# Masking the scores of the first block's attention with four passes on quarters of the rows

## The reference

```python
q = (x @ wq).reshape(b, n, H, DH)...   # 16 heads of 64
sim = jnp.einsum('bhid,bhjd->bhij', q, k) * SCALE
sim = jnp.where(mask[:, None, None, :], neg, sim)   # mask: 32 x 128, one flag for a key
attn = jax.nn.softmax(sim, axis=-1)
out = jnp.einsum('bhij,bhjd->bhid', attn, v)
```

## Time and profile before

| | us |
|---|---|
| median of 3 executions | 2085.46 |
| lowest, highest | 2080.9, 2087.44 |
| the profiled execution | 2081.89 |
| its span (first to last instruction) | 2080.2 |
| PE busy in the span | 1893.0 (91%) |
| PE's weight loads busy | 1501.7 (72%) |
| DVE, ACT, POOL busy | 1429.1, 1191.3, 498.9 |

### The profile page before, as it was taken

How to read it: one execution, slowest core, us unless ns; L and a number is a source line. 1 busy time by engine, 2 the same in 40 slices (tenths; PEclk the granted TensorE clock), 3 DMA queues, 4 the chain that set the end, 5 groups by cost and what they waited for, 6 DMA issues and landing times.

```text
span 2080.2 us, 47917 instructions
## 1 busy us (share of the span) xinstructions
PE 1893.0 (91%) x17007; PEld 1501.7 (72%) x17007; DVE 1429.1 (69%) x3597; ACT 1191.3 (57%) x3980; POOL 498.9 (24%) x810
## 2 busy tenths in 40 slices
PE   3899999999999999999599999888887788699998
PEld 1788888888888888888367777666665555467776
DVE  5577787777777777777465676478887699354443
ACT  1567676767676666776244544377776566133333
POOL 1021111111111111111221221044444576021110
PEclk8899999999999999999799999899999899599999
DMA  7000000000000000000200000100000000000000
GB/s 225 25 2 2 2 2 2 2 2 2 2 2 2 2 2 2 2 2 2 72 1 1 1 1 1 36 2 3 2 2 9 24 13 2 1 0 11 11 3 19
DMA packets 30226, 25.69 MB, mean 12 GB/s; under 512 B 5276, under 2 KB 26788, under 8 KB 29992
## 3 DMA queue, kind: packets, MB, share of 16 engines
q1 hardware_dynamic: 29992, 22.62, 3.7%
HBM read 20.52 MB, written 2.10 MB: 11 GB/s over the span
## 4 chain that ended last, share of the span: by engine, by line
issue 66%; POOL 15%; PE 10%; POOLq 8%; DVE 1%; DMA 0%; DVEq 0%; ACT 0%
POOL X L1797 3%; POOL work L914 2%; PE bank L1918 2%; PE bank L1905 2%; PE bank L1907 2%; POOL work L1588 2%; POOLq L917 2%; POOL H L918 1%; POOL work L1013 1%; POOL X L1598 1%; PE bank L1885 1%; POOLq L1587 1%; POOL work L902 1%; POOLq L1796 1%; POOLq L1597 1%
## 5 line engine op out<-in xcount | busy, mean ns | idle before, releaser
L679 ACT ACTIVATE work<-bank,work 128x128 f32<-128x128 f32 x1024 | 363.1, 402 | 208.2 <-DVE work L758 208.2
L520 PE MATMUL bank<-work,wbig 128*128 128x128 f32 x2048 | 262.3, 277 | 0.5 <-ACT work L742 0.5
L520 PEld LDWEIGHTS bank<-work,wbig 128*128 128x128 f32 x2048 | 246.0, 193 | 1.2 <-ACT work L742 0.8
L679 ACT ACTIVATION_READ_ACCUMULATOR work<-bank,work 128x1 f32 x1024 | 246.4, 241 | 0.0
L765 DVE TENSOR_TENSOR work<-work 128x512 f32<-128x512 f32 x256 | 177.7, 694 | 19.8 <-issue 0.9
L758 DVE TENSOR_REDUCE work<-bank 128x4 f32<-128x512 f32 x256 | 159.0, 684 | 33.6 <-PE bank L559 33.6
L694 ACT ACTIVATE work<-bank 128x512 f32<-128x512 f32 x256 | 168.7, 660 | 22.8 <-PE bank L533 22.8
L533 PE MATMUL bank<-ident,work 128*128 128x128 f32 x1024 | 157.6, 276 | 11.8 <-DVE work L765 11.8
L533 PEld LDWEIGHTS bank<-ident,work 128*128 128x128 f32 x1024 | 114.2, 140 | 58.7 <-issue 31.3
L912 POOL TENSOR_TENSOR work<-work,lneps 128x1 f32<-128x1 f32 x64 | 15.3, 238 | 580.9 <-DVE work L875 580.9
L2078 DVE TENSOR_TENSOR work<-wff,bank 128x320 f32<-128x320 f32 (+1 forms) x128 | 62.5, 489 | 127.7 <-ACT wff L1993 127.2
(11 more groups left out here) (311 smaller groups left out, 4016.6 us busy)
## 6 DMA issues: line engine op xcount, KB each, us to landing
wbig<-in_moe_w SPq DMA_DIRECT2D x2, 1536.0 KB, 9.3
work<-in_mask_l SPq DMA_DIRECT2D x8, 256.0 KB, 3.0
out<-X SPq DMA_DIRECT2D x8, 256.0 KB, 2.3
H<-in_moe_w SPq DMA_DIRECT2D x3, 512.0 KB, 5.6
wff<-in_moe_w SPq DMA_DIRECT2D x1, 1024.0 KB
X<-in_x SPq DMA_DIRECT2D x1, 512.0 KB, 4.1
wbig<-in_sa_wq SPq DMA_DIRECT2D x1, 512.0 KB, 3.9
wbig<-in_sa_wk SPq DMA_DIRECT2D x1, 512.0 KB, 4.7
```

Of the source, the lines that this page charges most:

```text
L520: last = nc.tensor.matmul(o[:, j * T:(j + 1) * T], w[:, t * 128:(t + 1) * 128], src, start=True, stop=True)
L679: last = nc.scalar.activation(at_probs[:, g, h, :], bank[g][:, h * T:(h + 1) * T], ACT.Exp, bias=at_nmax[:, g, h:h + 1], accum_out=at_den[ ...
```

## The change

The mask passes leave `score` and stand in a function `mask(u)` of their own, called once for a unit ahead of both calls of `score`. It does four passes, one for each of the four banks, each on a quarter of the rows (32 rows from partition 0, 32, 64, 96). The wait for the exponentials of the unit before (`at.probs` at 4u) stands ahead of them; the wait at 4u - 2 goes. For this `onerow` has a row of ones at the head of each quarter (four memsets for two), and `keymask` is filled on all partitions: the two halves of the mask are loaded onto all 128 partitions (two transfers for four), converted by two instructions on 128 partitions (for four on one), and the clearing of `keymask` goes. The rows of `keymask` under the zero rows of `onerow` no longer are zero.

```diff
-        mask32 = [[H[p:p + 1, NB * j:NB * j + NB, :].rearrange("p b d -> p (b d)").bitcast(mybir.dt.int32)
-                   for j in range(2)] for p in (0, DH0)]
-        mask8 = [[m.bitcast(mybir.dt.uint8) for m in pair] for pair in mask32]
+        mask32 = [H[:, NB * j:NB * j + NB, :].rearrange("p b d -> p (b d)").bitcast(mybir.dt.int32) for j in range(2)]
+        mask8 = [m.bitcast(mybir.dt.uint8) for m in mask32]
...
+            def mask(u):
+                b = unit(u)[1]
+                for g in range(GH):
+                    p = 32 * g
+                    nc.tensor.matmul(bank[g][:, :].rearrange("p (h t) -> p h t", h=GH), onerow[p:p + 32, :],
+                                     keymask[p:p + 32, b * T:(b + 1) * T].unsqueeze(1).to_broadcast([32, GH, T]),
+                                     start=True, stop=False, skip_group_check=True)
+
             def score(u, pair):
-                b = unit(u)[1]
-                for odd in range(2):
-                    p = odd * DH0
-                    nc.tensor.matmul(bank[2 * pair + odd][:, :].rearrange("p (h t) -> p h t", h=GH),
-                                     onerow[p:p + DH0, :],
-                                     keymask[p:p + DH0, b * T:(b + 1) * T].unsqueeze(1).to_broadcast([DH0, GH, T]),
-                                     start=True, stop=False, skip_group_check=True)
...
                 if now:
+                    need(pe, at.probs, 4 * u)
+                    mask(u)
                     need(pe, at.q_low_sb, u + 1)
                     need(pe, at.qk_sb, 3 * u + 3)
-                    need(pe, at.probs, 4 * u - 2)
                     score(u, 0)
-                    need(pe, at.probs, 4 * u)
                     score(u, 1)
...
-            for p in range(2):
-                for j in range(2):
-                    load(mask32[p][j], ins["mask"][:, j * B * T // 8:(j + 1) * B * T // 8], "mask")
+            for j in range(2):
+                load(mask32[j], ins["mask"][:, j * B * T // 8:(j + 1) * B * T // 8].to_broadcast([128, B * T // 8]), "mask")
...
             nc.gpsimd.memset(onerow[:, :], 0.0)
-            nc.gpsimd.memset(keymask[:, :], 0.0)
             nc.gpsimd.memset(b2_sb[:, :], 0.0)
             pool.drain()
-            nc.gpsimd.memset(onerow[0:1, :], 1.0)
-            nc.gpsimd.memset(onerow[DH0:DH0 + 1, :], 1.0)
+            for p in range(0, 128, 32):
+                nc.gpsimd.memset(onerow[p:p + 1, :], 1.0)
...
-            dve.wait_ge(loaded["mask"], 64)
-            for p in range(2):
-                for j in range(2):
-                    nc.vector.tensor_scalar(keymask[p * DH0:p * DH0 + 1, j * B * T // 2:(j + 1) * B * T // 2],
-                                            mask8[p][j], MASKED, None, ALU.mult)
+            dve.wait_ge(loaded["mask"], 32)
+            for j in range(2):
+                nc.vector.tensor_scalar(keymask[:, j * B * T // 2:(j + 1) * B * T // 2], mask8[j], MASKED, None, ALU.mult)
```

## The result

The changed kernel takes 2089.14 us (median of 20 executions, 2086.96 to 2090.49). The kernel before, run beside it as often, takes 2082.85 (2080.9 to 2087.55). The ratio is 1.0024 [1.0018, 1.0031]: some 5 us slower by the ratio, 6.3 by the two medians. That is inside the predicted range (2077 to 2096), 0.4 us from the predicted 2088.7, and within 0.3% of no change, the case that had the highest chance. The profiled execution took 2086.96 us with a span of 2085.2, against 2081.89 and 2080.2.

The account below looks back on a forecast made before the run. It took the path over DVE and ACT from score(u, 0) to the value product to pace most attention units, DVE's chain 23. Attention +7.1 us and preparation -2.3 make +4.8 on 2083.9: 2088.7 us, range 2077 to 2096.

Parts of the forecast that it names:

- the case that had the highest chance: Whole kernel: time within 0.3% (6.3 us) of no change, given 62%, against 29% slower and 9% faster.
- Which kinds of unit, and the path: Attention: units paced by ACT lose 0.17 to 0.2 us each, 23 paced by DVE hide the delay; PE's stream changes -0.01.
- The group of four passes, and the change of rows: Mask passes before the scores: four abreast take 0.22 us, plus 0.01 issue; going from 32 to 64 rows costs 0.20.
- ACT's slack of 0.02 us: ACT's copy of turn 0: 0.02 us of room absorbs part of the 0.21 us delay, leaving 0.19 in 18 units.
- The cover of the units paced by DVE: In 23 units, idle time of 0.43 and 0.45 us hides the 0.21 us delay; together they change by -0.2 us.
- The preparation at the barrier: Start of the kernel: without the clearing of keymask the barrier opens 2.3 us earlier, with 2.0 and 2.5 as ends.
- Nothing later absorbs it: After the start: the 2.3 us won reach the end, since stage 1 begins on DVE's end of stage 0, not a transfer.
- The sum: Whole kernel: attention +7.1 us and preparation -2.3 us give +4.8 us, set on the mean of 2083.9 us.
- (1): Rival, between masks and scores: changing from 32 to 64 rows causes no standstill; -6.5 us, 2077.4 us; 12%.
- (2): Rival, mask group: the four passes run two by two, 0.22 us longer in all 64 units; +18.9 us, 2102.8 us; 6%.
- (4): Rival, attention: the path over ACT doesn't carry the delay, PE's stream sets the pace; -2.9 us, 2081.0 us; 10%.
- (3): Rival, preparation: the start brings nothing because larger mask transfers hold back "mix" or RWKV weights; +7.1 us, 2091.0 us; 10%.

Follow-up runs that it names:

- The removed passes: The kernel before without the mask passes of score's second call: 2077.31 us, 0.9968; likewise without the first call's passes: 2075.04 us, 0.9956.
- the attention alone: The changed kernel's mask and score, with keymask cleared as in the kernel before and the mask loaded on four single partitions: 2091.41 us, 1.0036.
- the three copies of the preparation: The kernel before with the new mask loads, conversions and memsets, without clearing keymask, score untouched, run three times: ratios 0.9992, 0.9997, 0.9997.

## Why the prediction was right, and where its terms were off

*Which kinds of unit, and the path.* Right. ACT's path carries the delay in 40 units, DVE's units hide it, and PE's stream alone changes by -0.01 us. The removed passes confirm it from the other side.

*The group of four passes, and the change of rows.* Right to 0.01 us: 0.22 for the group, 0.10 of standstill, 0.10 of f32 weights in the open. The bounds were 0 and 0.20, and both neighbours in the trace were rightly taken over. The run with 32 rows in the second call shows each part by itself.

*ACT's slack of 0.02 us.* Wrong, and this is the larger part of the attention's miss (7.1 predicted; 8.0 in the trace, 7.4 with the attention alone). ACT did start its copy of turn 0 closer behind its neighbours. But where its instructions stand close, they are shown longer and longer (0.37 us for the first exponential of the unit, 0.43 for the twelfth), and the copy of piece 2 behind the closed gap is shown with 0.72 us instead of 0.68. The start moved and the end didn't. From the end of `score(u, 0)` to the value product it is 8.27 us where it was 8.25. So the delay passes as 0.22 and not as 0.19, and in the odd units, the stray 0.34 us of unit 7 left out, as 0.19 and not as 0.17: 18 x 0.03 + 22 x 0.02 = 1.0 us. A difference this small is near the scatter of the traces: of the three copies of the preparation, which are one program, two have units paced by ACT 0.02 us longer than the kernel before, and one has not.

*The cover of the units paced by DVE.* The waits behave as stated, but the -0.2 us for all of them together was mis-sized. I gave these units PE's -0.01 (23 x -0.01 = -0.2), and they measured -0.46 with one stray wait of -0.35 in it, so -0.1. No error that matters.

*The preparation at the barrier.* Predicted -2.3 us, with 2.0 and 2.5 as ends; it was -3.0, outside of both. Two steps failed. I took DVE's own end at 10.05 as a possible bound and let it shorten only a little. It went to 9.08 (ACT's work ends at 9.13), as its first scaling instructions had been held by nine memsets of other tiles that the clearing of `keymask` had pushed beside them (1.54 to 0.29 us). And I let ACT wait for the "mix" transfers at 7.26. ACT's table load, which is the longest part of its work (1.28 us), stands ahead of that wait and started at 6.75.

*"Nothing later absorbs it".* This step failed for the preparation alone. In its three copies PE began 3.0 us earlier and the first scores 3.0 to 3.9 us, and at the end of the program about 1 us was left. The prediction looked for a transfer or an engine that could be late next, and there was none. What moved was the granted clock of stages that the change doesn't touch, up to 1700 us later. In the changed kernel itself less was absorbed: its trace has 3.9 us at the first scores and gives back 0.9 behind the last ones.

*The sum.* Predicted +4.8 = 7.1 - 2.3. There are two ways to take the measured sum apart, and they disagree on the start. By the separate kernels it is +7.4 (attention alone) - 1.0 (preparation alone) = +6.4, as the two medians say (+6.3); then the attention was 0.3 us too low, the start brought 1.3 us less than the sum had, and both errors go the same way. By the changed kernel's own trace it is +8.0 (the periods) - 3.0 (3.9 won ahead of them, 0.9 lost behind) = +5.0, as the ratio says (3.7 to 6.5); then the attention was 0.9 us too low and the start brought 0.7 us more than the sum had, so that two errors cancel. The changed kernel against the attention alone (1.0024 and 1.0036, on two chips, with intervals that overlap) is 2.5 us for a start of PE 3.4 us earlier, nearer to the second. The runs don't settle it. The level of 2083.9 on which the sum was set is the mean of the kernel before (2083.8 over its 20 executions) and 1 us above its median. The mechanism of the attention was right; that 2088.7 and 2089.14 lie only 0.4 us apart is in part luck either way.

*The rivals.* (1), no standstill, is ruled out by the rows of the changed kernel and of the one with 32 rows in the second call, (2) by the row of 0.40 us for four passes, (4) by the run without the second passes. Of (3) the cause is ruled out, as the larger mask transfers hold nothing back at the barrier; its size, a start that brings nothing, is 1.0 us from what the copies of the preparation kept and 3.0 us from what the changed kernel's trace shows.

## What to carry to other kernels

An instruction packed away is worth nothing if it stood behind the work that the next engine waits for, and the change costs if it puts any of it ahead: sum the stream and the path to each consumer apart. Passes on another number of rows than their neighbours cost 0.10 us of standstill at each change and, where f32 weights follow, 0.10 more: as much as the 0.22 us that packing four instead of two abreast saves, so pack only where a whole stretch of work has the same row count. A few microseconds won at the start of a program with stretches at the lower clock are to be measured at its end and over many executions: the kernel before took 2082.9 us in executions with a mean clock of 0.963 and 2085.7 at 0.960, and a single trace falls on one of them.

## What was not expected of the hardware

- Passes on bf16 weights between a change of rows and the f32 products hid the first f32 load: without them the sixteen score instructions took 1.00 us instead of 0.89.
- The costs of a change of rows are the same in both directions, 64 to 32 and 32 to 64: 0.10 us each.
- DVE's scaling instructions of 0.28 us, when begun beside POOL's memsets, ended 0.07 to 0.08 us after the last of these and not before: the first of them took 1.54 and 2.00 us beside nine short memsets, 2.23 beside one of 3.51 us.
- The time at the lower clock late in the program differs between kernels whose late stages are the same: 126.3 to 139.4 us over fourteen traces, and that part of the program is up to 5.4 us longer with it. Open: what decides it. An earlier start alone doesn't, and whether a start earlier by yet another amount would be paid back wasn't tried.
